# Attention and gated network on one core: a row of zeros for the maxima's products, and four groups of instructions in other places

## The chip, the cores and the metric

The kernel runs on one NeuronCore of a Trainium2 chip. The metric is the device time of one execution in microseconds; 677.85 us is the median of three runs (677.08 to 679.14). The engines have short names: PE is TensorE (PEld its weight loads), DVE VectorE, ACT ScalarE, POOL GpSimd, SP SyncE, which issues all transfers.

## The reference

For x of 4 x 512 x 512, the layer norm xn feeds two branches that are multiplied:

```
xn = (x - mean) / sqrt(var + 1e-5)
q, k, v = split(xn @ w_qkv)            # 16 heads of 32
q, k = rope(rmsnorm(q)*q_gamma), rope(rmsnorm(k)*k_gamma)
s = softmax(causal(q k^T / sqrt(32))) v @ w_out
f = (silu(xn Wg^T) * (xn Wu^T)) Wd^T   # hidden 1408, W = (int - 128)*scale
out = x + s * silu(f)
```

All of it is float32 in and out. The products on PE take a number as a high and a low part.

## The kernel before, in words

**Beats.** The middle of the program is 65 beats; beat c (0 to 63) does the attention of one head of one group of four heads: batch c // 16, group c // 4 % 4, head k = c % 4. Each engine has a written-out list of steps for a beat (`beat`), and goes through it in order; steps of different engines are tied by semaphores alone. In beat c, PE makes the transposed scores of head c in three operations (`scores_t`, L1383), the products with v of head c-1 and the first of head c (`p_v`, L1398), the products for the row maxima of block k of the next group (`maxima`, L1419, four heads), the projection of tile c+7 (`project`, L1358), the turns of tile c+5 (`turn`, L1370, for q and then k, both through one bank) and up to two halves of the gate and up products (`gate_half`, L1461).

**Maxima.** A softmax needs the maximum of a row first. q and k of a head stand as three parts of 32 rows each (KS = 96 rows) in `qst` and `kst`. The maxima's products use these 96 rows. Row 96 of `qst` holds the negated maxima, written there by SP's transfers `m0_out` and `m_out`, and row 96 of `kst` holds ones, so that the scores, with 97 rows, come out less the maximum. On DVE `maxima` (L1094) reduces a bank; PE may use a bank again when DVE is through with it.

**Statistics.** Where `ln_at` says so, DVE's beat has `ln_stats` (L1015 to L1021) and `ln_apply` (L1027) for one tile of the next batch, with POOL's power (L631) between them. They stand behind the last maxima of the beat and ahead of the sum of the rope (L1061) and of `p_low` of operation 2 (L1072). Before, they are in beats 2, 4, 6, 8 for batch 1, in 16, 18, 20, 22 for batch 2, in 32, 34, 36, 38 for batch 3. PE turns these tiles in beats 9 and 10 (batch 1), 23 to 26 and 39 to 42, whose output goes to both branches.

**Down products.** From beat 57 on PE also does `down`: 22 products a tile, two for each of 11 pieces m of the hidden size (L1486, L1487), into banks 0 to 3. `DOWN_AT` puts them at the end of a beat. In beats 55 to 58 PE also has the output projection of batch 2 (`out_proj`, L1437), 12 products in three parts through the same bank as the turns, so that the turn of q waits for ACT's `s_evac` (L811) and the turn of k for ACT's `q_evac` (L771).

**The ending.** Behind the beats PE does the rest of the down products, tiles n = 3 to 15 (n = 4b + t), and between them the four output projections of the last batch. The pieces of a tile become usable in chunks (four, four and three pieces): a load `hf_raw` by SP (L397), a high part on ACT (L853), a low part on DVE (L1140). DVE's order there is fixed too: low(9), scaled(0,2), o_low, low(10), scaled(0,3), finish(0,0), finish(0,1), low(11) and so on; low(10) and low(11) are the chunks of tile (1, 2) from m = 4 and from m = 8. A `finish` (L1279, L1281) needs its `xs` loads and a free half of `res`; SP then stores it.

## Time and profile before

| | |
|---|---|
| median of the runs | 677.85 us (677.08 to 679.14) |
| the profiled execution | 678.34 us, its span 676.6 us |
| PE, PEld | busy 652.6 us (96%), 551.5 us (82%) |
| DVE, ACT, POOL | busy 536.0 us (79%), 456.5 us (67%), 414.8 us (61%) |
| chain that ended last | PE 69%, DVE 11%, POOL 5%, issue 5%, DMA 5%, ACT 4% |
| granted clock, mean | 0.997 |
| DMA | 94.40 MB, 140 GB/s |

The span is the time from the first to the last instruction of one profiled execution; its 678.34 us holds 1.7 us more around it. The granted clock is the share of TensorE's full clock that it was given.

### The profile page before, as it was taken

How to read it: one execution, taken by the hardware profiler on the slowest of the kernel's cores; microseconds unless marked ns; L12 is line 12 of the kernel's file. 1: busy time of each engine (PE TensorE's matmuls, PEld its weight loads, DVE VectorE, ACT ScalarE, POOL GpSimd, SP SyncE). 2: the span in 40 equal slices, each digit the busy share in tenths (PEclk: the TensorE clock that was granted, in tenths of full speed). 3: DMA queues.
4: the chain of work that ended last, by engine and by line, in shares of the span. 5: the costliest groups of instructions: out<-in, count | busy, mean ns of one | idle time of the engine just before them, and what ended most of it. 6: DMA issues, size and time to landing. Idle time of an engine off the chain costs nothing.

```text
span 676.6 us, 12576 instructions
## 1 busy us (share of the span) xinstructions
PE 652.6 (96%) x3690; PEld 551.5 (82%) x3690; DVE 536.0 (79%) x1345; ACT 456.5 (67%) x1013; POOL 414.8 (61%) x591
## 2 busy tenths in 40 slices
PE   8889999999999999999999999999999989999997
PEld 7778888888888878888888888888888876777786
DVE  6786988998798888787988887878788866735857
ACT  3588787877676767776766677777677765741541
POOL 7968787787666667676666676766657673520000
PEclk9999999999999999999999999999999989999999
DMA  7546436332524341154343421244462515449896
GB/s 278 194 140 216 152 125 187 105 106 79 154 73 134 103 111 49 48 157 125 111 126 95 110 65 45 73 113 150 121 202 79 156 42 155 119 143 333 281 325 202
DMA packets 62591, 94.40 MB, mean 140 GB/s; under 512 B 12092, under 2 KB 24380, under 8 KB 62396
## 3 DMA queue, kind: packets, MB, share of 16 engines
q1 hardware_dynamic: 62524, 93.59, 45.0%
q8 instruction: 31, 0.51, 0.3%
q14 instruction: 36, 0.29, 0.2%
HBM read 59.09 MB, written 25.82 MB: 125 GB/s over the span
## 4 chain that ended last, share of the span: by engine, by line
PE 69%; DVE 11%; POOL 5%; issue 5%; DMA 5%; ACT 4%; SPq 1%; DVEq 0%; ACTq 0%; POOLq 0%
PE bank L1461 22%; PE bank L1358 16%; PE bank L1398 9%; PE bank L1419 5%; PE bank L1383 4%; PE bank L1370 4%; PE bank L1437 4%; DMA hf_raw<-hf_dram 2%; DVE bank L1094 2%; DVE ht_l L1140 2%; POOL rr L635 1%; ACT ht_h L853 1%; DMA out<-res 1%; PE bank L1486 1%; PE bank L1487 1%
## 5 line engine op out<-in xcount | busy, mean ns | idle before, releaser
L655 POOL TENSOR_SCALAR_AFFINE_SELECT pp<-pp 128x256 fp32r<-128x256 f32 x256 | 108.2, 435 | 141.1 <-DVE pp L1072 140.9
L1094 DVE CUSTOM_DVE_ANT_0 bank<-bank,msk_w 128x128 f32<-128x128 f32 (+3 forms) x256 | 121.3, 510 | 41.6 <-PE bank L1419 41.5
L1072 DVE TENSOR_TENSOR pp<-pf,pp 128x512 fp32r<-128x512 f32 (+1 forms) x192 | 135.4, 705 | 5.1 <-ACT pp L786 4.5
L635 POOL TENSOR_TENSOR rr<-ss,half 128x8 f32<-128x8 f32 x64 | 109.5, 1712 | 17.0 <-DVE ss L1040 17.0
L1358 PE MATMUL bank<-wq,xnt_h 128*128 128x384 f32 x512 | 111.7, 340 | 2.7 <-DVE qn L1052 2.4
L785 ACT ACTIVATE pf<-bank 128x512 f32<-128x512 f32 (+1 forms) x192 | 100.4, 523 | 19.5 <-PE bank L1383 17.3
L786 ACT ACTIVATE pp<-bank 128x512 fp32r<-128x512 f32 (+1 forms) x192 | 100.8, 525 | 0.0
L1461 PE MATMUL bank<-xnt_h,wgu 128*128 128x512 f32 x352 | 99.0, 403 | 0.7 <-DVE g L1118 0.7
L1398 PE MATMUL bank<-pp,va 128*65 128x512 f32 (+3 forms) x512 | 97.5, 311 | 1.0 <-POOL pp L655 1.0
L1461 PE MATMUL bank<-xnt_l,wgu 128*128 128x512 f32 x352 | 96.6, 396 | 0.0
L1358 PEld LDWEIGHTS bank<-wq,xnt_h 128*128 128x128 f32 x512 | 88.4, 188 | 6.0 <-issue 4.2
L1461 PEld LDWEIGHTS bank<-xnt_l,wgu 128*128 128x128 f32 x352 | 66.2, 188 | 16.3
L644 POOL TENSOR_TENSOR rb<-qn,sg 128x128 f32<-128x128 f32 x128 | 72.3, 585 | 0.0
L1419 PE MATMUL bank<-kst,qst 96*128 96x128 f32 (+3 forms) x256 | 71.2, 349 | 1.0 <-DVE mx L1094 0.8
L1486 PE MATMUL bank<-wd,ht_h 128*128 128x512 f32 (+1 forms) x187 | 70.9, 384 | 1.3 <-DVE ht_l L1140 1.1
L1398 PEld LDWEIGHTS bank<-pp,va 128*65 128x65 f32 x512 | 58.4, 136 | 16.8 <-POOL pp L655 1.4
L1487 PE MATMUL bank<-wd,ht_l 128*128 128x512 f32 (+1 forms) x187 | 70.6, 383 | 0.0
L1461 PEld LDWEIGHTS bank<-xnt_h,wgu 128*128 128x128 f32 x352 | 60.8, 188 | 11.4 <-issue 1.1
L1358 PE MATMUL bank<-wq,xnt_l 128*128 128x384 f32 x256 | 69.0, 352 | 0.0
L776 ACT ACTIVATE kst<-bank 96x512 fp32r<-96x512 f32 x64 | 38.0, 593 | 40.9 <-PE bank L1370 40.9
L771 ACT ACTIVATE qst<-bank 96x512 fp32r<-96x512 f32 x64 | 38.1, 595 | 39.1 <-PE bank L1370 39.0
L1370 PEld LDWEIGHTS bank<-idr,tt 128*96 128x96 f32 x512 | 49.0, 125 | 18.4 <-issue 3.8
(90 smaller groups left out, 1210.3 us busy)
## 6 DMA issues: line engine op xcount, KB each, us to landing
wgu<-wg_dram SPq DMA_DIRECT2D x66, 256.0 KB, 3.1
hf_dram<-g SPq DMA_DIRECT2D x44, 256.0 KB, 3.2
hf_raw<-hf_dram SPq DMA_DIRECT2D x16, 512.0 KB, 6.9
wg_dram<-wgu SPq DMA_DIRECT2D x22, 256.0 KB, 3.1
xr<-x SPq DMA_DIRECT2D x16, 256.0 KB, 4.6
oh<-oraw SPq DMA_DIRECT2D x64, 64.0 KB, 2.0
ol<-oraw SPq DMA_DIRECT2D x64, 64.0 KB, 2.0
s_dram<-s_sb SPq DMA_DIRECT2D x16, 256.0 KB, 2.7
```

Source lines behind the costliest of these rows:

```text
L635: pool.tensor_tensor(rr[:, s, :], ss[:, s, :], half[:], ALU.pow).then_inc(rr_ok, 1)
L655: op = pool.affine_select(pp[:, :, a:a + P], pp[:, :, a:a + P], [[0, 2], [1, P]], ALU.is_ge, 0.0, base=0, channel_multiplier=-1)
L785: act.activation(pf[:, tile], bank[:, 0:w], ACT.Exp, scale=SCALE)
L786: act.activation(ph[:, tile], bank[:, 0:w], ACT.Exp, scale=SCALE).then_inc(p_ok, 1)
L1072: dve.tensor_tensor(pl[:, tile], pf[:, tile], ph[:, tile].bitcast(F32), ALU.subtract).then_inc(pl_ok, 1)
L1094: op = dve.tensor_tensor_reduce(bank[:, a * w:(a + 1) * w], bank[:, a * w:(a + 1) * w], msk_w[:, N - w:N], 1.0, -3.0e38, ALU.add, ALU.max, ...
L1358: op = pe.matmul(qkv_bank(n)[:, 0:3 * GC], x_[:, k, t * P:(t + 1) * P], wq[:, g, w_, k, :], start=(a == 0), stop=(a == len(todo) - 1))
L1398: op = pe.matmul(PV_PS[0:VW, j * P:N], va[:, v, j, h, :], part[:, a:a + w], start=(j == 0 and part is ph), stop=(j == 2 and part is pl))
L1419: op = pe.matmul(bank[:, a * w:(a + 1) * w], qst[0:KS, par, h, qb * P:(qb + 1) * P], kst[0:KS, par, h, 0:w], start=True, stop=True)
L1461: op = pe.matmul(GU_PS[:], wgu[:, s, k, :], x_[:, k, :], start=(a == 0), stop=(a == len(todo) - 1))
L1486: pe.matmul(down_bank(t, part)[:, out_], ht_h[s][:, m, cols], wd[:, m, out_], start=(m == 0), stop=False)
L1487: op = pe.matmul(down_bank(t, part)[:, out_], ht_l[s][:, m, cols], wd[:, m, out_], start=False, stop=(m == MT - 1))
```

## The change

1. `KM = KS + 1`. Row 96 of `qst` becomes zeros (one transfer in the fill), rows 96 and 97 of `kst` ones, and the negated maxima go to row 97. The maxima's products take 97 rows (zero times one is added), the scores 98. PE waits for the zeros ahead of its first maxima.
2. `ln_at`: the statistics are in beats 4, 5, 7, 8 for batch 1, 12, 16, 20, 24 for batch 2, 28, 32, 36, 40 for batch 3; the load of the tiles is one beat earlier.
3. `DOWN_MID`: the four pieces of beat 57 and the four of beat 58 go in pairs ahead of the turn of q and ahead of the turn of k.
4. The four late output projections stand behind tiles 6 to 9, not 5 to 8, with ACT's and SP's steps for them; SP issues the first three chunks of batch 2 right behind the first `xs` loads.

```
+KM = KS + 1
+        DOWN_MID = {57: ((0, 0, 2), (0, 2, 4)), 58: ((0, 4, 6), (0, 6, 8))}
-        DOWN_AT = {57: ((0, 0, 4),), 58: ((0, 4, 8),), 59: ((0, 8, MT), (1, 0, 3)), 60: ((1, 3, 8),),
+        DOWN_AT = {59: ((0, 8, MT), (1, 0, 3)), 60: ((1, 3, 8),),
@@ ln_at
-            b, t = r + 1 + c // 16, c % 16 - (0 if c // 16 else 2)
-            t = t // 2 if t in (0, 2, 4, 6) else None
+            b = (c + 4) // 16 + 1
+            t = (c + 4) % 16 // 4 if c % 4 == 0 else None
+            if b == 1 or c == 0:
+                b, t = 1, {4: 0, 5: 1, 7: 2, 8: 3}.get(c)
@@ sync: m0_out, and m_out likewise; beat; fill; the ending
-                sp.dma_start(qst[KS:KS + 1, par, 0:1, :].bitcast(F32).rearrange(
+                sp.dma_start(qst[KM:KM + 1, par, 0:1, :].bitcast(F32).rearrange(
-                if c % 16 == 12 and there(c // 16 + 2, B):
+                if c % 16 == 11 and there(c // 16 + 2, B):
+                sp.wait_ge(zero_ok, 1)
+                sp.dma_start(qst[KS:KM, :, :, :].bitcast(F32).rearrange("o a h n -> o (a h) n"),
+                             pp[0:2 * HG, 0, 0:N].bitcast(F32)).then_inc(zr_in, 16)
                 load_w(1)
...
             for t in range(TB):
                 load_xs(0, t)
+            sp.wait_ge(dn_full, TB)
+            for v in range(NC):
+                load_hf(4 * NC + v)
...
-                    for v in range(2 * NC):
+                    for v in range(NC if b == 1 else 0, 2 * NC):
-                if TB + 1 < n <= 2 * TB + 1:
-                    s_store(B - 1, n - TB - 2)
+                if TB + 2 < n <= 2 * TB + 2:
+                    s_store(B - 1, n - TB - 3)
@@ gpsimd
-            pool.memset(kst[KS:KS + 1, :, :, :].bitcast(F32), 1.0).then_inc(ones_ok, 1)
+            pool.memset(kst[KS:KM + 1, :, :, :].bitcast(F32), 1.0).then_inc(ones_ok, 1)
@@ scalar: the ending
-                if TB < n <= 2 * TB:
-                    s_evac(B - 1, n - TB - 1, LATE_PS[n - TB - 1])
+                if TB + 1 < n <= 2 * TB + 1:
+                    s_evac(B - 1, n - TB - 2, LATE_PS[n - TB - 2])
@@ tensor: scores_t, maxima, beat, fill, the ending
-                    op = pe.matmul(bank[:, c0:c0 + w], kst[0:KS + 1, par, h, j * P:(j + 1) * P],
+                    op = pe.matmul(bank[:, c0:c0 + w], kst[0:KM + 1, par, h, j * P:(j + 1) * P],
...
-                        op = pe.matmul(bank[:, a * w:(a + 1) * w], qst[0:KS, par, h, qb * P:(qb + 1) * P],
-                                       kst[0:KS, par, h, 0:w], start=True, stop=True)
+                        op = pe.matmul(bank[:, a * w:(a + 1) * w], qst[0:KM, par, h, qb * P:(qb + 1) * P],
+                                       kst[0:KM, par, h, 0:w], start=True, stop=True)
+                if c in DOWN_MID:
+                    down(0, *DOWN_MID[c][0])
                 turn_q()
...
+                if c in DOWN_MID:
+                    down(0, *DOWN_MID[c][1])
                 if late_turn(c):
                     turn_k()
...
+                pe.wait_ge(zr_in, 16)
                 maxima(0, 0, (0,))
...
-                if TB < n <= 2 * TB:
-                    late = n - TB - 1
+                if TB + 1 < n <= 2 * TB + 1:
+                    late = n - TB - 2
```

How the order of instructions moves. On PE in beat 57, from the scores of operation 2 on (L1437 is the output projection, L1370 the turns, L1486 and L1487 the down products), before:

```order
L1383 MATMUL bank<-qst,kst 128x256
L1437 MATMUL bank<-wo_h,on 128x512
L1437 MATMUL bank<-wo_h,on_l 128x512 x3
L1370 MATMUL bank<-idr,tt 96x128 x8
L1486 MATMUL bank<-wd,ht_h 128x512
L1487 MATMUL bank<-wd,ht_l 128x512
L1486 MATMUL bank<-wd,ht_h 128x512
```

and in the changed kernel, where the same lines are L1393, L1447, L1380, L1496 and L1497:

```order
L1393 MATMUL bank<-qst,kst 128x256
L1447 MATMUL bank<-wo_h,on 128x512
L1447 MATMUL bank<-wo_h,on_l 128x512 x3
L1496 MATMUL bank<-wd,ht_h 128x512
L1497 MATMUL bank<-wd,ht_l 128x512
L1496 MATMUL bank<-wd,ht_h 128x512
L1497 MATMUL bank<-wd,ht_l 128x512
L1380 MATMUL bank<-idr,tt 96x128 x4
L1496 MATMUL bank<-wd,ht_h 128x512
L1497 MATMUL bank<-wd,ht_l 128x512
```

Two down pieces now stand ahead of the turn of q and two between the turns. On DVE in beat 7, from the last maxima to the next gate step (L1061 sums the rope, L1072 makes the low part of operation 2), before:

```order
L1094 ISA bank,mx<-bank,msk_w 128x512
L1094 ISA mx 128x1
L1061 TENSOR_TENSOR qp<-ra,rb 128x256
L1072 TENSOR_TENSOR pp<-pf,pp 128x256
L1040 TENSOR_REDUCE ss<-sq 128x8
L1123 SCALAR_TENSOR_TENSOR g<-bank,hsc,g 128x512
```

and in the changed kernel (L1104 maxima, L1071 rope, L1082 low part, L1050 squares, L1133 gate step):

```order
L1104 ISA bank,mx<-bank,msk_w 128x512
L1104 ISA mx 128x1
L1025 BN_STATS st<-xr 128x6
L1028 COPY st<-st 128x1
L1029 BN_AGGR mv<-st 128x2
L1031 TENSOR_SCALAR ve<-mv 128x1
L1071 TENSOR_TENSOR qp<-ra,rb 128x256
L1082 TENSOR_TENSOR pp<-pf,pp 128x256
L1037 TENSOR_SCALAR xr<-xr,mv,rstd 128x512
L1050 TENSOR_REDUCE ss<-sq 128x8
L1133 SCALAR_TENSOR_TENSOR g<-bank,hsc,g 128x512
```

The statistics of tile 2 have come between them from beat 6. On SP in the ending, from the last load of batch 0's `xs` on, before (L542 `xs`, L547 the stores, L397 the chunks):

```order
L542 DMA xs<-s_dram 128x512
L547 DMA out<-res 128x512
L542 DMA xs<-x 128x512
```

and in the changed kernel (L549, L401, L554):

```order
L549 DMA xs<-s_dram 128x512
L401 DMA hf_raw<-hf_dram 128x4x256 x2
L401 DMA hf_raw<-hf_dram 128x3x256
L554 DMA out<-res 128x512
L549 DMA xs<-x 128x512
```

The three chunks stood behind three stores before, and stand ahead of the first now.

## Rows read from the trace of the kernel before

**Rows 1.** Windows: length, busy PE, PEld, DVE, ACT, POOL (x), PEclk, DMA share, GB/s.
```profile
82.00:242.00 160.00, 157.86 (x937) 135.55 (x936) 138.83 (x373) 120.20 (x278) 115.95 (x164) 1.00 0.40 119
126.92:133.89 6.97, 6.14 (x45) 5.57 (x44) 6.50 (x19) 5.38 (x12) 4.28 (x7) 1.00 0.23 78
176.05:185.40 9.35, 9.35 (x54) 7.91 (x53) 7.53 (x19) 6.27 (x15) 5.56 (x10) 1.00 0.37 114
212.08:222.02 9.94, 9.61 (x54) 7.91 (x53) 8.57 (x23) 6.71 (x17) 6.80 (x11) 1.00 0.33 113
246.82:256.64 9.82, 8.95 (x54) 7.62 (x53) 8.72 (x24) 6.04 (x15) 7.19 (x10) 1.00 0.26 81
```

**Rows 2.** Groups by form on PE: form, count, busy us, mean ns, idle before.
```profile
L1419 PE MATMUL bank<-kst,qst 96*128 96x512 f32 x64 | 25.6, 438 | 0.8 <-DVE mx L1094 0.8
L1419 PE MATMUL bank<-kst,qst 96*128 96x384 f32 x64 | 21.1, 370 | 0.0
L1419 PE MATMUL bank<-kst,qst 96*128 96x256 f32 x64 | 14.3, 307 | 0.0
L1419 PE MATMUL bank<-kst,qst 96*128 96x128 f32 x64 | 10.3, 283 | 0.2 <-ACT kst L776 0.2
L1383 PE MATMUL bank<-qst,kst 97*128 97x512 f32 x64 | 25.4, 398 | 0.0
L1383 PE MATMUL bank<-qst,kst 97*128 97x384 f32 x64 | 21.7, 339 | 0.0
L1383 PE MATMUL bank<-qst,kst 97*128 97x256 f32 x64 | 19.2, 299 | 0.6 <-ACT pp L786 0.5
L1383 PE MATMUL bank<-qst,kst 97*128 97x128 f32 x64 | 14.3, 223 | 0.0
```

**Rows 3.** Timeline, PE, turn of beats 55 and 56: start us, length us, instruction.
```profile
535.91 0.41 PE L1370 MATMUL bank<-idr,tt 128*96 128x128 f32 x4
536.16 0.64 PE L1398 MATMUL bank<-pp,va 128*65 128x512 f32 x2
537.24 0.63 PE L1419 MATMUL bank<-kst,qst 96*128 96x128 f32 x4
537.71 0.51 PE L1398 MATMUL bank<-pp,va 128*65 128x384 f32 x2
```

**Rows 4.** Groups by form on DVE: the statistics and their application.
```profile
L1015 DVE BATCH_NORM_STATS2 st<-xr 128x6 f32<-128x512 f32 x16 | 11.0, 686 | 1.9 <-DMA xr<-x 1.9
L1027 DVE TENSOR_SCALAR xr<-xr,mv,rstd 128x512 f32<-128x512 f32 x16 | 9.9, 620 | 2.4 <-POOL rstd L607 0.9
```

**Rows 5.** Waits of PE between 545 and 566 us: total, times, longest.
```profile
PE bank L1370 <- ACT s_sb L811: 1.7, 2, 1.0
PE bank L1370 <- ACT qst L771: 1.1, 2, 0.8
```

**Rows 6.** Windows within beat 57, before and in the fall of the clock.
```profile
549.93:553.20 3.27, 1.51 (x11) 1.17 (x11) 2.92 (x5) 2.07 (x6) 3.27 (x5) 1.00 0.02 5
553.20:556.60 3.40, 3.40 (x10) 2.39 (x9) 0.71 (x2) 0.84 (x3) 1.76 (x2) 0.52 0.15 37
```

**Rows 7.** Timeline, PE, the first two late output projections.
```profile
608.24 1.17 PE L1437 MATMUL bank<-wo_h,on_h 128*128 128x512 f32 x4 [1.24 <-ACT on_h L799]
616.58 1.09 PE L1437 MATMUL bank<-wo_h,on_h 128*128 128x512 f32 x4
```

**Rows 8.** Timeline, DVE, two low parts of the ending and the tail.
```profile
609.08 1.22 DVE L1140 TENSOR_TENSOR ht_l<-hf_raw,ht_h 128x1024 fp32r<-128x1024 f32 x1 [0.26 <-ACT ht_h L853]
614.08 0.95 DVE L1140 TENSOR_TENSOR ht_l<-hf_raw,ht_h 128x768 fp32r<-128x768 f32 x1
671.08 0.69 DVE L1279 TENSOR_TENSOR res<-gt,xs 128x512 f32<-128x512 f32 x1 [1.59 <-DMA out<-res]
```

**Rows 9.** Waits of PE from 590 us on.
```profile
PE bank L1486 <- DVE ht_l L1140: 1.1, 2, 1.0
```

**Rows 10.** The page, DMA issues.
```profile
oh<-oraw SPq DMA_DIRECT2D x64, 64.0 KB, 2.0
```

More of the change, by code:

```diff
@@ L191, in build @@
         hf_raw = (hf_raw0, hf_raw1, hf_raw2, hf_raw3)
-        zero_ok = sem("zero_ok")
+        zero_ok, zr_in = sem("zero_ok"), sem("zr_in")
         id_in, c_in, msk_in = sem("id_in"), sem("c_in"), sem("msk_in")
@@ L442, in m_out @@
                 sp.wait_ge(mt_ok, 4 * r + c // 4 + 1)
-                sp.dma_start(qst[KS:KS + 1, par, 1:HG, :].bitcast(F32).rearrange(
+                sp.dma_start(qst[KM:KM + 1, par, 1:HG, :].bitcast(F32).rearrange(
                     "o h (t n) -> o (h t) n", t=TB), mrow[:].bitcast(F32)).then_inc(m_in, 16)
@@ L1382, in scores_t @@
                 for j, c0, w in ST_OPS[e]:
-                    op = pe.matmul(bank[:, c0:c0 + w], kst[0:KS + 1, par, h, j * P:(j + 1) * P],
-                                   qst[0:KS + 1, par, h, j * P:N], start=True, stop=True)
+                    op = pe.matmul(bank[:, c0:c0 + w], kst[0:KM + 1, par, h, j * P:(j + 1) * P],
+                                   qst[0:KM + 1, par, h, j * P:N], start=True, stop=True)
                 op.then_inc(st_full, 1)
```

## The prediction

> **What bounds the kernel now.** I read the windows first. From 82 to 242 us PE is busy 157.86 of 160 us and no other engine over 139 (the first row) [rows 1]. So in the beats the time is PE's list of products and how tightly they follow each other, and a product made shorter is time gained. The exceptions are in the same group: beat 9 (126.92 to 133.89), where PE is busy 6.14 of 6.97 us; beat 19 (212.08 to 222.02), 9.94 us long where beat 15 (176.05), with nearly the same products, takes 9.35; and beat 23 (246.82), where PE idles 0.87 of 9.82 us. Then the groups by form, to set the maxima's products beside the scores; then PE's waits and the clock in beats 57 and 58; then the ending, where the order of PE and the lateness of DVE's low parts decide.
>
> **The 97th row.** 256 products on PE change, 64 of each width. With 96 rows they take 438, 370, 307 and 283 ns for 512, 384, 256 and 128 columns; the scores, with 97 rows and the same widths, take 398, 339, 299 and 223 [rows 2]. The scores show no extra time where they precede or follow products of 128 rows, so I expect the maxima to become like them: 64 x (40 + 31 + 8 + 60) ns = 8.9 us. Durations of pipelined products overlap, so the starts are a second bound: four maxima of 128 columns take 0.47 us from the first start to the next group's (537.24 to 537.71), four turns of 128 columns and 128 rows take 0.25 (535.91 to 536.16), 0.055 us each more [rows 3]; on all 256 that is 14 us. The low end is 0, if the row count isn't the cause; a loss I exclude, since the scores carry a 97th row and are the shorter ones. I take 8.9 us, since the wide ones show less than the narrow ones. The scores go from 97 to 98 rows, at no cost: both lie within what the 97 rows already need beyond 96. The transfer of zeros is one of some 2.0 us [rows 10], issued in the fill among loads of much more, and its wait stands ahead of the first maxima, behind five tiles' projections; behind that wait all of PE's list is queued, so if the cover were gone it would cost the 2.0 us. SP's wait for the zeros in SBUF holds the load of weights behind it, for a clearing on which PE's first products wait anyway.
>
> The Trainium skill, page "TensorE: Matmul & The Clock Gate", section "LDWEIGHTS (loading the stationary operand)", says that a load takes its time from the columns and that fewer contraction rows don't change it, and its section "Why this matters for your kernels" gives a product of 32 rows the same time as one of 128. By that rule this term is 0. The rows of the trace disagree for products of 96 rows, and I go by the rows.
>
> **The statistics.** One tile costs DVE 0.69 us for the statistics and 0.62 for their application [rows 4], 1.3 us with the three small steps left out. Taken away: in beats 2, 18 and 34 they make DVE late for the heavy beat that follows; beat 19 is 9.94 - 9.35 = 0.59 us longer than beat 15, whose forerunner has none [rows 1]. Three such beats give 1.8 us. In beats 22 and 38 they stand before beats 23 and 39, where PE idles 0.87 us [rows 1]: 1.7 us. Added: tile 2 of batch 1 goes from beat 6 to beat 7, where DVE is loaded most, with beat 8's behind it and beats 9 and 10 ahead, in which PE waits for DVE already. Nothing there hides 1.3 us on DVE, so PE pays 1.3; at best 0, if DVE gains as much in beat 7 from what left beat 6. Beats 12 and 28 get one after a short beat; I put down 0.3 each, between 0 and 1.3. Queued behind the statistics on DVE are the rope's sum and the low part of operation 2, for which POOL's mask and PE's products wait a beat later. Beats 24 and 40 cost nothing: PE has output projections there and DVE half a beat's rest. Sum -3.5 + 1.9 = -1.6, between -3.5 and +1.7.
>
> **The down products of beats 57 and 58.** PE waits 1.7 us in two waits for ACT's copy of the output projection and 1.1 in two for the copy of the turned q [rows 5]. In each place now stand four products. A product of 512 columns takes (616.58 - 608.24 - 0.3) / 34 = 0.236 us (12 of the projection, 22 down, and a short wait between) [rows 7], so four take 0.94: as much as the longest wait. What they need (the last projection's bank, the first chunks) is there a beat before. 2.7 of the 2.8 us go. With them goes the reason for the fall of the clock: in 549.93 to 553.20 PE is busy 1.51 of 3.27 us, and in the 3.40 us that follow the granted clock is 0.52, that is the 1.2 GHz level for nearly all of it, in which PE loses (1 - 0.52) x 3.40 = 1.6 us [rows 6]. Sum -4.3, between -2.0 and -4.5. What is late next is POOL's mask for the products with v, some tenths behind.
>
> **The ending.** Before, PE is through with tile (1, 1) at 608.24 - 1.24 = 607.0 and waits for the last group's output, then does the projection, 12 x 0.236 = 2.8 us, then tile (1, 2), until 616.58 [rows 7]. Now tile (1, 2) starts at 607.0. Its pieces from m = 4 are at hand at 609.08 + 1.22 = 610.3, those from m = 8 at 614.08 + 0.95 = 615.0 [rows 8]; DVE's and ACT's order there, and the loads that this hangs on, don't change. So 8 products until 608.9, a wait of 1.4, 8 products until 612.2, a wait of 2.8, 6 products until 616.4. PE is where it was, without the 2.8 us of projection: +2.6. The waits of 1.1 us for low parts [rows 9], of which 1.0 is the start of tile (2, 0), go, since its chunks are now loaded three stores earlier: -1.0. DVE is then less behind, and its wait of 1.59 us for a store in the tail [rows 8] shrinks; 0.6 of it is on the end's path by my estimate (0 to 1.6). And from 608.9 to 615.0 PE would be busy 1.9 of 6.1 us, 31%, less than the 46% ahead of the fall in beat 57 [rows 6]: I expect the clock to fall here, for +1.6. Sum +2.6 - 1.0 - 0.6 + 1.6 = +2.6, between -1.6 (the low parts come sooner with a less crowded queue) and +3.5.
>
> **The sum.** -8.9 - 1.6 - 4.3 + 2.6 = -12.2 us, from 678.34 of the profiled execution: 666.1. That execution is 0.5 us over the median of the runs shown, so 665.6.
>
> **Rivals.** *The clock holds in the ending* (its fall in beat 57 is one event, and single waits of 1.2 us did not bring one): 1.6 less, 664.0. *DVE takes PE's place.* The beats get 0.14 us shorter each while DVE's work stays; in beats 7 to 12 and wherever DVE fills over 8.5 us it becomes the bound, and half of the 8.9 does not arrive: 670.1. For it speaks beat 19 [rows 1], against it the 21 us of DVE's rest in 160. *The row count is not the cause*: the maxima are long because each waits for a bank that DVE has just left. Then 8.9 us are missing: 674.5. Against it: products behind each other in one bank, with no wait between, are long as well [rows 3]. *Slower than before*: the two waits of the ending drop the clock to 1.2 GHz and it stays there through the following 55 us of down products, where PE is the bound; that would lose half, up to 27 us, and from 24 us of it the kernel is slower than 677.85: 680 or so. Against it: in beat 57 it came back within 3.40 us of dense products [rows 6]. *More than the durations show*: at the 14 us of the starts, 661.
>
> **Chances.** Forecast 0.45 (its own range 664.8 to 667.5), clock holds 0.22, DVE 0.18, row count 0.08, slower 0.02, more 0.05. The range 661 to 671.5 leaves out the row count, the slow case and the edges of the DVE case. A measurement of this kernel tells about 0.3%, 2 us, from no change; all cases but one lie further down: faster 0.97, same 0.01, slower 0.02.
>
> **What would show it.** By form: the maxima at 398, 339, 299 and 223 ns, within 10. Beats 19 and 35 at 9.4 us, 23 and 39 at 9.0, beats 9 and 10 together a us longer. No wait at the turns of beats 57 and 58, beat 57 near 7.8 us, clock 1.00. In the ending two waits for low parts in tile (1, 2), of over 1 and over 2 us, with a window of clock near 0.5 right behind, and none at tile (2, 0). I am wrong if the maxima keep their durations, if waits for DVE grow by over 4 us in the beats, or if tile (1, 2) finds its low parts ready.

## The result: 0.4% faster, where 1.8% was forecast

The changed kernel takes 674.91 us, median of 7 runs (674.32 to 676.46), against 677.14 for the kernel before in the same session (7 runs, 676.41 to 679.14). The ratio is 0.9963, 95% interval 0.9951 to 0.9975, so 1.7 to 3.3 us faster. The forecast was 665.6 us with a range from 661 to 671.5: the time lies outside it. The profiled execution took 675.65 us with a span of 673.9.

First the groups by form on PE, the question of the largest term. In this view a row has the form (rows * columns of the weights, then rows x width of the moving side), the count, the busy time, the mean ns and the idle time before:

```profile
L1429 PE MATMUL bank<-kst,qst 97*128 97x512 f32 x64 | 25.6, 438 | 0.8 <-DVE mx L1104 0.8
L1429 PE MATMUL bank<-kst,qst 97*128 97x384 f32 x64 | 21.2, 371 | 0.0
L1429 PE MATMUL bank<-kst,qst 97*128 97x256 f32 x64 | 14.3, 307 | 0.0
L1429 PE MATMUL bank<-kst,qst 97*128 97x128 f32 x64 | 10.3, 283 | 0.2 <-ACT kst L786 0.2
L1393 PE MATMUL bank<-qst,kst 98*128 98x512 f32 x64 | 25.6, 401 | 0.0
```

They answer to [rows 2]: the maxima now have 97 rows and take 438, 371, 307 and 283 ns, where they took 438, 370, 307 and 283 with 96. Not one nanosecond of 8.9 us came.

Then the windows (length, busy PE, PEld, DVE, ACT, POOL, granted clock, DMA share, GB/s): 160 us of beats, and beats 9, 15, 19 and 23, which answer to [rows 1]:

```profile
83.72:243.72 160.00, 157.84 (x934) 135.06 (x933) 137.96 (x378) 120.07 (x276) 114.02 (x164) 1.00 0.41 117
129.10:136.07 6.97, 6.27 (x46) 5.57 (x45) 6.67 (x19) 5.39 (x13) 4.41 (x7) 1.00 0.24 78
178.40:187.80 9.40, 9.40 (x55) 7.94 (x54) 7.53 (x19) 6.28 (x15) 5.58 (x10) 1.00 0.38 121
214.47:223.86 9.39, 9.39 (x55) 7.93 (x54) 7.28 (x19) 6.68 (x16) 5.59 (x10) 1.00 0.39 111
248.70:257.48 8.78, 8.78 (x55) 7.66 (x54) 7.12 (x19) 6.01 (x15) 6.38 (x9) 1.00 0.30 85
```

PE is as full as before. Beat 9 has its old length, beat 19 is now 9.39 us long (9.94 before), beat 23 8.78 (9.82 before), and PE no longer idles in it.

In beats 57 and 58 the waits of [rows 5] are gone: between 545 and 566 us PE's waits are two of 0.2 us. Beat 57 takes 7.80 us instead of 11.24, beat 58 7.73 instead of 9.34. The place of the fall of the clock in [rows 6] reads 1.00. The fall stands elsewhere now, twice: in the fill, and in the ending. The rows are beat 57, the fill, and the ending before and in its fall:

```profile
553.00:556.50 3.50, 3.50 (x21) 2.97 (x20) 2.82 (x7) 3.03 (x8) 1.86 (x3) 1.00 0.18 40
44.50:48.00 3.50, 3.50 (x12) 2.79 (x11) 2.02 (x7) 1.44 (x5) 2.14 (x2) 0.51 0.45 150
604.90:611.10 6.20, 3.33 (x13) 2.44 (x14) 4.79 (x8) 1.98 (x3) 0.00 (x0) 1.00 1.06 384
611.20:614.60 3.40, 3.40 (x10) 2.64 (x9) 0.00 (x0) 0.00 (x0) 0.00 (x0) 0.50 1.09 376
```

The ending answers to [rows 7 to 9]. First PE's timeline at its two waits in tile (1, 2) and the projection behind them, then ScalarE's (ACT) and VectorE's (DVE) at the same place (start, length, instruction, in brackets the idle time before it and what ended it), then PE's waits from 584 us on (total, times, longest):

```profile
604.98 0.50 PE L1496 MATMUL bank<-wd,ht_h 128*128 128x512 f32 x1 [1.51 <-DVE ht_l L1150]
609.91 0.50 PE L1496 MATMUL bank<-wd,ht_h 128*128 128x512 f32 x1 [2.79 <-DVE ht_l L1150]
611.61 1.91 PE L1447 MATMUL bank<-wo_h,on_h 128*128 128x512 f32 x4
```
```profile
601.94 0.63 ACT L809 ACTIVATE on_h<-on 128x512 fp32r<-128x512 f32 x1 [2.52 <-POOL on L678]
602.61 1.06 ACT L863 ACTIVATE ht_h<-hf_raw 128x1024 fp32r<-128x1024 f32 x1
603.70 1.23 DVE L1150 TENSOR_TENSOR ht_l<-hf_raw,ht_h 128x1024 fp32r<-128x1024 f32 x1 [0.40 <-ACT ht_h L863]
606.22 0.69 DVE L1289 TENSOR_TENSOR res<-gt,xs 128x512 f32<-128x512 f32 x1 [0.70 <-DMA xs<-s_dram]
607.00 0.63 ACT L869 ACTIVATE gt<-yt 128x512 f32<-128x512 f32 x1 [3.34 <-DVE res L1289]
607.54 0.83 ACT L863 ACTIVATE ht_h<-hf_raw 128x768 fp32r<-128x768 f32 x1
608.90 0.95 DVE L1150 TENSOR_TENSOR ht_l<-hf_raw,ht_h 128x768 fp32r<-128x768 f32 x1
```
```profile
PE bank L1496 <- DVE ht_l L1150: 4.5, 3, 2.8
```

Both waits have a queue behind them. The second chunk's high half on ACT (602.61) stands in order behind the copy of the last normalized block, which waits 2.52 us for POOL. The third chunk's low half on DVE (608.90) stands behind the residual sums of tiles (0, 0) and (0, 1), which wait for a DMA. Its high half on ACT (607.54) is queued too: it stands behind an activation that waits 3.34 us for the first of these sums. PE's four projections then take 1.91 us instead of 1.17, the clock having fallen.

The account of the profiled executions, by the start of beats: beat 0 starts 1.40 us later (47.16 against 45.76), beats 0 to 62 take 534.11 instead of 541.03 us (-6.92), and from beat 63 to the end it is 92.64 instead of 89.83 (+2.81). The sum is -2.7 us, as the spans say. The +2.81 are +3.6 until PE's last product and -0.8 from there to the end (4.26 us instead of 5.04).

### The profile page after: what moved, and what is told of

Its sections match the earlier page's. It is cut to its first block, busy times and chain, and to the rows that moved or that the text cites. A ratio compares the mean times of both kernels' runs of the same rounds, so it can differ in the third digit from the quotient of the medians.

```text
span 673.9 us, 12577 instructions
## 1 busy us (share of the span) xinstructions
PE 653.6 (97%) x3690; PEld 553.1 (82%) x3690; DVE 531.5 (79%) x1345; ACT 456.9 (68%) x1013; POOL 412.3 (61%) x591
## 4 chain that ended last, share of the span: by engine, by line
PE 81%; DVE 5%; POOL 5%; ACT 3%; issue 3%; DMA 2%; SPq 1%; ACTq 0%; DVEq 0%; POOLq 0%
PE bank L1471 23%; PE bank L1368 17%; PE bank L1408 9%; PE bank L1447 6%; PE bank L1429 6%; PE bank L1393 5%; PE bank L1497 4%; PE bank L1496 4%; PE bank L1380 4%; POOL rr L645 1%; DMA stage<-w_qkv 1%; DVE bank L1104 1%; POOL pp L665 1%; DVE pp L1082 1%; DMA xs<-s_dram 1%
## 5 line engine op out<-in xcount | busy, mean ns | idle before, releaser
L1104 DVE CUSTOM_DVE_ANT_0 bank<-bank,msk_w 128x128 f32<-128x128 f32 (+3 forms) x256 | 121.3, 509 | 38.2 <-PE bank L1429 37.8
L1082 DVE TENSOR_TENSOR pp<-pf,pp 128x512 fp32r<-128x512 f32 (+1 forms) x192 | 133.0, 693 | 5.0 <-ACT pp L796 4.4
L1496 PE MATMUL bank<-wd,ht_h 128*128 128x512 f32 (+1 forms) x187 | 70.3, 381 | 4.5 <-DVE ht_l L1150 4.5
L1429 PE MATMUL bank<-kst,qst 97*128 97x128 f32 (+3 forms) x256 | 71.3, 350 | 1.0 <-DVE mx L1104 0.8
L1497 PE MATMUL bank<-wd,ht_l 128*128 128x512 f32 (+1 forms) x187 | 70.3, 382 | 0.0
L1380 PEld LDWEIGHTS bank<-idr,tt 128*96 128x96 f32 x512 | 49.1, 125 | 15.2 <-issue 2.4
```

Of the source, the lines that this page charges most:

```text
L1082: dve.tensor_tensor(pl[:, tile], pf[:, tile], ph[:, tile].bitcast(F32), ALU.subtract).then_inc(pl_ok, 1)
L1104: op = dve.tensor_tensor_reduce(bank[:, a * w:(a + 1) * w], bank[:, a * w:(a + 1) * w], msk_w[:, N - w:N], 1.0, -3.0e38, ALU.add, ALU.max, ...
L1429: op = pe.matmul(bank[:, a * w:(a + 1) * w], qst[0:KM, par, h, qb * P:(qb + 1) * P], kst[0:KM, par, h, 0:w], start=True, stop=True)
L1496: pe.matmul(down_bank(t, part)[:, out_], ht_h[s][:, m, cols], wd[:, m, out_], start=(m == 0), stop=False)
L1497: op = pe.matmul(down_bank(t, part)[:, out_], ht_l[s][:, m, cols], wd[:, m, out_], start=False, stop=(m == MT - 1))
```

## The experiments

Each is measured beside the kernel before on the same chip. The interval in brackets is that of the ratio. Of each edit only the main lines are shown.

**The parts one by one.** The row of zeros alone:

```
+KM = KS + 1        # maxima 97 rows, scores 98, statistic in row KM
+                sp.dma_start(qst[KS:KM, :, :, :]..., pp[0:2 * HG, 0, 0:N]...).then_inc(zr_in, 16)
```


> The kernel before with the row of zeros alone (scores 98 rows, maxima 97 rows, the statistic of the maxima moved to row 97, the transfer of zeros in the fill and the wait for it). Theory of the prediction (rows set the pace of a maxima product): the 512-wide maxima fall from 438 to about 400 ns and the kernel is 8.9 us faster. Theory now (the row count sets nothing; what is slow is the product that stands behind a 128-wide one, whatever its rows): maxima products stay at 438, 371, 307 and 283 ns within 5 ns, and the time is the one before, or up to 1.6 us longer if the clock falls in the fill at 44 to 48 us as in the changed kernel. If the clock does not fall in the fill here, the row of zeros is not its cause, and the loss of 1.4 us before beat 0 belongs to another part.

Measured: 677.96 against 677.16 us, ratio 1.0006 (0.9993 to 1.0020). The durations:

```profile
L1423 PE MATMUL bank<-kst,qst 97*128 97x512 f32 x64 | 25.6, 438 | 0.8 <-DVE mx L1098 0.8
L1423 PE MATMUL bank<-kst,qst 97*128 97x128 f32 x64 | 10.3, 283 | 0.2 <-ACT kst L780 0.2
```

The part does nothing to the products. The clock didn't fall in the fill in this execution. It did in that of the late projections alone (below), where the row is left out, so the row of zeros is not needed for the fall:

```profile
44.50:47.90 3.40, 3.40 (x12) 2.75 (x10) 2.01 (x8) 1.44 (x4) 1.99 (x2) 0.51 0.47 154
```

The statistics alone:

```
-            t = t // 2 if t in (0, 2, 4, 6) else None
+            t = (c + 4) % 16 // 4 if c % 4 == 0 else None
+            if b == 1 or c == 0:
+                b, t = 1, {4: 0, 5: 1, 7: 2, 8: 3}.get(c)
```


> The kernel before with the places of the statistics alone (and the load of the next block's rows one beat earlier). My forecast of this part was 1.6 us faster; the lengths of beats in the trace of the changed kernel against those of the kernel before now say about 2.3 us faster (beats 3, 19, 35 each 0.5 to 0.6 and beats 23, 39 each 1.0 to 1.1 shorter, beat 6 longer by 1.0, beats 8, 13, 29 by 0.2 each). If that reading is right, 1.8 to 2.8 us come off with the statistics alone; the rival, that the gains of the changed kernel come from the row of zeros and its shorter waits, expects under 1 us here.

Measured: 676.77 us, ratio 0.9984 (0.9967 to 1.0001), that is 1.1 us faster, between 2.2 faster and 0.1 slower: by the runs alone not clear of no change. The beats that changed are those of the changed kernel to 0.04 us: 3, 19 and 35 shorter by 0.50 to 0.62, 23 and 39 by 1.05 and 1.09, beat 6 longer by 0.92, beats 8, 13, 29 by 0.17 to 0.19, in sum -2.4. So the gains belong to the statistics and not to the row, as the first theory had it. One beat runs against it: beat 60 is 0.84 us longer in this execution, with a wait of 0.7 us of its scores for the transfer of the maxima. That wait is absent in the changed kernel, so it isn't the statistics' own, but it leaves 1.5 us over the beats. The median's smaller gain also fits its runs' lower clock, 0.9959 in the mean against 0.9979 (the table below).

The down products alone:

```
+        DOWN_MID = {57: ((0, 0, 2), (0, 2, 4)), 58: ((0, 4, 6), (0, 6, 8))}
+                if c in DOWN_MID:
+                    down(0, *DOWN_MID[c][0])
                 turn_q()
```


> The kernel before with the down products of beats 57 and 58 in four pieces inside the beats alone. Forecast 4.3 us faster; the trace of the changed kernel says 5.0 us over beats 57 and 58, with no stretch at half clock at 553 to 557. Expected here: 4.3 to 5.1 us faster, clock fall of 553 to 557 gone. The rival, that the waits come back in beats 59 to 63 (VectorE is what feeds them), expects under 2.5 us.

Measured: 673.75 us, ratio 0.9947 (0.9928 to 0.9965), 2.4 to 4.9 us faster, the largest part, though its 3.6 us lie under the 4.3 to 5.1 that I expected. Beats 57 and 58 are 7.79 and 7.76 us. Beat 59 is 0.66 us longer than before, and 0.5 of it is a wait of the scores for the transfer of the maxima:

```profile
PE bank L1384 <- DMA qst<-mrow: 0.5, 1, 0.5
```

Other executions with the new order have this wait with 0.3 to 0.7 us, the changed kernel's has none, and the statistics alone have it in beat 60 with the old order. So I can't put it down to the down products. It is far less than the rival asked for.

The ending alone, with ACT's and SP's steps and the three early loads:

```
-                if TB < n <= 2 * TB:
-                    late = n - TB - 1
+                if TB + 1 < n <= 2 * TB + 1:
+                    late = n - TB - 2
```


> The kernel before with the ending alone: the last block's output projections one tile later, their evacuations and stores with them, and the three early loads of block 2's halves. Forecast 2.6 us slower, and the trace of the changed kernel says 2.7 us: TensorE waits for VectorE's low halves in the second and third tile of the ending (1.5 and 2.8 us, in place of 1.1 and 2.0), and the clock is halved for about 3.4 us behind them. If the projections' move is what does it, this kernel is 2.2 to 3.2 us slower than before and shows a stretch at half clock in the ending. The rival, that the early end of beats 57 and 58 is what makes VectorE late in the ending (it has the same work in less time), expects this kernel within 1 us of the one before.

Measured: 679.83 us, ratio 1.0035 (1.0017 to 1.0052), 1.2 to 3.5 us slower. PE's waits in its trace after 588 us:

```profile
PE bank L1489 <- DVE ht_l L1143: 4.1, 3, 2.2
```

The waits come with this part alone; that beats 57 and 58 end earlier isn't needed for them. In this execution the clock held in the ending in spite of them, so the stretch at half clock that I expected was not seen here; its one fall before the end was in the fill.

The other way round, the changed kernel with the projections where they were; the early loads stay:

```
-                if TB + 1 < n <= 2 * TB + 1:
-                    late = n - TB - 2
+                if TB < n <= 2 * TB:
+                    late = n - TB - 1
```


> The changed kernel with the output projections of the ending where they were before (one tile earlier); all else of the change stays, the row of zeros among it. If the parts add up as measured one by one (later projections 2.4 us slower), this is 672.5 us, within 671.5 to 673.5. If the ending of the changed kernel is slow for another reason (VectorE late from beats 57 and 58), it is within 0.7 us of the changed kernel's 674.9.

Measured: 670.95 us, ratio 0.9917 (0.9897 to 0.9936). By the ratios that is 3.1 us under the changed kernel (4.0 by the medians of the two sessions), and 1.5 us better than I expected from the single parts. The 2.4 us of the ending alone are the move and the early loads together, the 3.1 are the move alone; the intervals are too wide to read the loads' worth from the difference. PE waits 1.1 us once in its ending, for the last normalized block:

```profile
PE bank L1447 <- ACT on_h L809: 1.1, 1, 1.1
```

So more than half of what the other parts gained, 5.6 us by this ratio, was given back by this one; with both intervals, the move cost about 1.5 to 4.7 us.

**What makes the maxima long.** The two scores of the second operation exchanged, in the kernel before:

```
-ST_OPS = [[(0, 0, 512)], [(1, 0, 384), (3, 384, 128)], [(2, 0, 256)]]
+ST_OPS = [[(0, 0, 512)], [(3, 384, 128), (1, 0, 384)], [(2, 0, 256)]]
```


> The kernel before with the two products of the second scores operation exchanged: the 128-wide one (queries of block 3) first, the 384-wide one behind it. Theory now (a product is late by 0.05 to 0.07 us when it loads 128 columns of weights behind a 128-wide product): the 512- and 384-wide maxima that stand directly behind the scores fall from 443 to about 398 ns and from 388 to about 341 ns, and the 384-wide score, now behind the 128-wide one, rises from 337 to about 385 ns; the time stays within 1.5 us of the one before. Rival (a maxima product is long by itself, by its 96 rows or because VectorE is still reading the neighbouring bank): maxima stay at 443 and 388 ns, scores at 337.

Measured: 677.54 us, ratio 1.0008 (0.9986 to 1.0031). By form:

```profile
L1383 PE MATMUL bank<-qst,kst 97*128 97x384 f32 x64 | 24.9, 389 | 0.0
L1419 PE MATMUL bank<-kst,qst 96*128 96x512 f32 x64 | 24.8, 426 | 0.8 <-DVE mx L1094 0.8
L1419 PE MATMUL bank<-kst,qst 96*128 96x384 f32 x64 | 20.4, 359 | 0.0
L1383 PE MATMUL bank<-qst,kst 97*128 97x128 f32 x64 | 14.3, 224 | 0.0
```

The 384-wide scores, always fast before (339 ns), are long now (389), because now they stand behind the 128-wide one. The maxima have become shorter without a change to their operands, by 12 ns in the mean of 64: a quarter of them stood directly behind the scores. Sorted by what stands ahead, the 512-wide maxima behind the scores go from 443 ns to 395, and those behind another 512-wide maximum stay (397 and 395). Beat 19's start shows one of these, first in the changed kernel, then in this one:

```profile
214.47 0.63 PE L1393 MATMUL bank<-qst,kst 98*128 98x512 f32 x3
214.94 0.44 PE L1429 MATMUL bank<-kst,qst 97*128 97x512 f32 x1
```
```profile
212.75 0.68 PE L1383 MATMUL bank<-qst,kst 97*128 97x512 f32 x3
213.27 0.39 PE L1419 MATMUL bank<-kst,qst 96*128 96x512 f32 x1
```

Three scores 0.63 us and the maximum 0.44; exchanged, 0.68 and 0.39. The 0.05 us belongs to the product that follows a 128-wide one, whichever that is. It was moved, not removed, and the time stayed. DVE reads the same banks in both kernels, so its reading isn't the cause.

The maxima with 96 instead of 128 columns of weights (the maxima of 32 queries in each block left out):

```
-    pe.matmul(bank[:, a * w:(a + 1) * w], qst[0:KS, par, h, qb * P:(qb + 1) * P],
+    pe.matmul(bank[0:KS, a * w:(a + 1) * w], qst[0:KS, par, h, qb * P:qb * P + KS],
```


> The kernel before with maxima of 96 query columns instead of 128 as the stationary operand (the maxima of 32 queries in each block are left out); rows, moving widths and order are as before. Theory now (loading 128 columns takes about 0.11 us, which a 128-wide product of 0.06 us does not cover): the group of four 128-wide maxima goes from a spacing of about 0.11 us to about 0.07 to 0.09, its products from 276 ns to about 240, and the maxima behind a 128-wide product fall by 0.02 to 0.04 us; those behind a 384- or 512-wide product stay at 341 and 398 ns. Rival (rows or VectorE's reading of the bank): nothing changes in these durations. The time: 0 to 1 us under the one before, too little to tell.

Measured: 675.97 us, ratio 0.9990 (0.9970 to 1.0009).

```profile
L1419 PE MATMUL bank<-kst,qst 96*96 96x512 f32 x64 | 24.7, 424 | 0.8 <-DVE mx L1094 0.8
L1419 PE MATMUL bank<-kst,qst 96*96 96x384 f32 x64 | 20.3, 358 | 0.0
L1419 PE MATMUL bank<-kst,qst 96*96 96x256 f32 x64 | 13.5, 295 | 0.0
L1419 PE MATMUL bank<-kst,qst 96*96 96x128 f32 x64 | 8.8, 261 | 0.2 <-ACT kst L776 0.2
```

With the same rows and fewer columns all four forms get shorter, by 12 to 22 ns. The gain sits behind the narrow products: behind the 128-wide score the 512-wide maximum goes from 443 to 419 ns, behind another 512-wide one it stays (397 and 398). The time's interval holds both no change and 2 us, as I had said it would be too small to tell. The group of four 128-wide maxima at the head of beat 20, PE and then the weight loads (PEld), in the changed kernel and in this one:

```profile
224.35 0.64 PE L1429 MATMUL bank<-kst,qst 97*128 97x128 f32 x4
224.32 0.53 PEld L1429 LDWEIGHTS bank<-kst,qst 97*128 97x128 f32 x4
```
```profile
221.55 0.56 PE L1419 MATMUL bank<-kst,qst 96*96 96x128 f32 x4
221.52 0.45 PEld L1419 LDWEIGHTS bank<-kst,qst 96*96 96x96 f32 x4
```

Over all such groups the starts of neighbouring 128-wide products are in the median 113 ns apart with 128 columns of weights and 96 or 97 rows, 109 with 128 columns and 128 rows (the transposes of x), 87 with 96 columns, 59 with 65 columns (the products with v). Columns set the pace of these products, rows don't. A 128-wide product passes in 59 ns or less; the load of 128 columns for the next one takes about 110, and the 50 ns between them show as lateness of that next one. Behind a product 256 wide or wider the load is covered: a 256-wide maximum takes 281 ns behind another 256-wide one and 332 behind the 128-wide score, a 512-wide maximum 397 to 399 ns behind a 384- or 512-wide product.

**What is worth keeping.** Down products and statistics, with batch 1's statistics at other beats and the early loads; the row and the late projections left out:

```
-                b, t = 1, {4: 0, 5: 1, 7: 2, 8: 3}.get(c)
+                b, t = 1, {1: 0, 4: 1, 6: 2, 8: 3}.get(c)
```


> What should be left of the change: the down products of beats 57 and 58 in pieces, the statistics at new places (those of batch 1 in beats 1, 4, 6 and 8 instead of 4, 5, 7 and 8, because the trace of the statistics alone shows beat 6 1.0 us longer), the early loads of block 2's halves; the row of zeros and the later output projections are left out. From the single parts measured (down 3.6 off, statistics 1.1 to 2.4 off and 0.9 more if beat 6 is as before) I expect 671.5, within 670 to 673; if VectorE's lateness simply comes back in the ending (rival), 673.5 or more, like the down products alone.

Measured: 670.01 us, ratio 0.9906 (0.9887 to 0.9925). I expected 671.5 from the single parts, within 670 to 673; as with the projections put back, the parts together gave 1.5 us more than their sum. Beat 6 is back at 8.99 us; beat 2 is 0.28 longer. PE's waits after 588 us:

```profile
PE bank L1443 <- ACT on_h L805: 1.5, 1, 1.5
PE bank L1492 <- DVE ht_l L1146: 0.2, 1, 0.2
```

On the same kernel, the first maxima of each beat behind the products with v, which load 65 columns:

```
-                banks(SM_A)
                 if k:
                     w_bank(0)
...
                     p_v(r, c - 1, 2)
+                banks(SM_A)
```


> The same kernel with the first maxima of each beat (the four 128-wide ones, or the first wider one) moved from behind the scores to behind the two value products of the beat before, whose weights are 65 columns wide. Theory now: the product behind the 128-wide score then loads 65 columns and is not late (the value product behind it stays at 408 or less), and the first maxima fall from 443 to about 400 ns; up to 60 times 0.05 = 3 us off against the kernel without this move, if VectorE, which gets these maxima about 1.5 us later, does not make TensorE wait for its low parts (that rival: 0 to 4 us slower, with waits for VectorE in front of the value products at the beat's end). Theory of rows: no product gets shorter and nothing is gained.

Measured: 678.62 us, ratio 1.0025 (1.0012 to 1.0039), 8.6 us slower than the kept version. By form between 183 and 320 us the 512-wide maxima take 418 ns against 436 in the kept version, the 128-wide ones 263 against 283. The v product that now stands behind the 128-wide score and loads 65 columns takes 341 ns, as behind wide ones (336): the mechanism is right. But these are PE's largest waits from 47 to 588 us, here and in the kept version:

```profile
PE bank L1404 <- POOL pp L661: 3.0, 6, 0.8
PE bank L1364 <- DVE qn L1058: 3.0, 5, 1.3
PE bank L1422 <- DVE mx L1100: 2.9, 4, 0.9
```
```profile
PE bank L1364 <- DVE qn L1058: 2.0, 3, 1.0
PE bank L1404 <- POOL pp L661: 0.9, 3, 0.3
```

The chain through DVE starts later and PE pays more for it than it saves: 18 of 63 beats get 0.2 to 0.9 us longer, and the beats together 7.8 us. The rival held, at twice the size that I gave it. The lists of waits, with their smaller rows, account for 5.2 us of this; the rest isn't traced.

**The queue in the ending.** Late projections again, on the kept version, with the second and third chunk's high halves on ACT and low halves on DVE ahead of what they stood behind, and SP's load of the second chunk ahead of the reciprocals' way back. ACT's lines:

```
             high(9)
-            o_high(LAST, G - 1)
             high(10)
-            outer(0, 2)
+            o_high(LAST, G - 1)
             high(11)
+            outer(0, 2)
```


> The kept version (670.0 us) with the later output projections of the changed kernel put in again, and three queues put in the order that these need: ScalarE makes the high halves of the second and third chunk of tiles (1,2), (1,3) ahead of the last normalized block's evacuation and the activations, VectorE makes their low halves ahead of the last block's low part and of the residual sums, SyncE issues the second chunk's load ahead of the last reciprocals' way back. Theory (the ending was slower because these products wait in order behind work that itself waits for GpSimd and for a DMA): the waits of 1.5 and 2.8 us in tile (1,2) go, TensorE no longer waits 1.5 us for the last normalized block either, and the time is 668.5, 1.5 us under the kept version. Rival (the loads of the second and third chunk are what comes late; they are issued at about 597 us): the waits in tile (1,2) stay at 1 us or more, and the time is 670.5 to 672.5. Up to 1 us is added if the clock falls behind such a wait.

Measured: 670.11 us, ratio 0.9904 (0.9885 to 0.9922), not the 668.5 that I expected: no faster than the kept version (0.9906, and 0.9894 when it was run again). The wait for the second chunk is gone, that for the third is 1.28 us instead of 2.79, and it stands behind the same copy as the second's did before:

```profile
602.41 0.63 ACT L805 ACTIVATE on_h<-on 128x512 fp32r<-128x512 f32 x1 [2.44 <-POOL on L674]
602.95 0.83 ACT L859 ACTIVATE ht_h<-hf_raw 128x768 fp32r<-128x768 f32 x1
604.83 0.50 PE L1492 MATMUL bank<-wd,ht_h 128*128 128x512 f32 x1 [1.28 <-DVE ht_l L1146]
```

With the third chunk ahead of it as well, on ACT and DVE, and its load on SP:

```
             high(10)
+            high(11)
             o_high(LAST, G - 1)
-            high(11)
```


> The kernel with the reordered ending, but now the third chunk of tiles (1,2), (1,3) too goes ahead of the last normalized block on ScalarE and VectorE, and its load ahead of the last reciprocals' way back on SyncE. The trace of the kernel before this step shows the one wait that is left in the ending, 1.28 us at 604.8 in tile (1,2) for the third chunk's low halves, behind an evacuation on ScalarE that starts at 602.4 when GpSimd is done. Theory: that wait goes to under 0.3 us and the time is 668.9, 1.1 to 1.3 us under the kept version on the same chip. Rival (the reciprocals' way back, now behind one more load, makes the last block late and TensorE waits for it in front of the output projections instead): 1 us or more of waiting for ScalarE there, and no gain.

Measured: 670.56 us, ratio 0.9909 (0.9892 to 0.9926), where I expected 668.9. That wait is gone, PE's only ones from 585 us on are

```profile
PE bank L1492 <- DVE ht_l L1146: 0.5, 2, 0.3
```

and the stretch from beat 63 to the end is 87.10 us against 87.85 and 87.98 in the kept version's two profiles. The time doesn't show these 0.8 us; here is the kept version again on the same chip:

> The kept version once more, beside the one above on the same chip: 670.0, within 0.7 us of its first time.

Measured: 669.63 us, ratio 0.9894 (0.9875 to 0.9912). By the medians the kernel with the late projections is 0.9 us slower than this, within the noise. That the waits go when the order of the queues and of one load, then two, is changed is shown. The queues and the loads were not changed apart; for the queues speaks that in the changed kernel both high halves start right behind other work on ACT and don't wait for a load. That the late projections are worth anything without the waits isn't shown.

**The clock.** The kept version's two profiles differ by 1.5 us in the span with the same instructions. The same stretch of the fill in the first and in the second:

```profile
44.00:47.50 3.50, 3.50 (x18) 2.98 (x19) 3.24 (x10) 2.85 (x6) 2.51 (x2) 1.00 0.32 110
```
```profile
44.00:47.50 3.50, 3.50 (x9) 2.79 (x10) 2.08 (x7) 1.93 (x4) 2.49 (x3) 0.51 0.38 105
```

So the fall in the fill, and the one in beat 57 of the kernel before, come in some executions and not in others: in the profile of the row of zeros alone beat 57 ran at full clock and took 9.74 us, not 11.24. Over the profiled executions of all kernels here, the fall in the fill is in 5 of 14. The one in beat 57 is in 3 of the 6 with the old order of the down products and in none of the 8 with the new one. The one in the ending is in that of the changed kernel alone. Mean granted clock and times, over the runs:

| kernel | runs | mean clock | mean us of the runs at 0.997 (how many) |
|---|---|---|---|
| before, beside the experiments | 79 | 0.9979 | 677.7 (30) |
| changed | 7 | 0.9944 | 674.5 (1) |
| row of zeros | 12 | 0.9974 | 678.2 (5) |
| statistics | 12 | 0.9959 | 675.9 (3) |
| down products | 6 | 0.9982 | 674.8 (1) |
| late projections | 12 | 0.9962 | 679.8 (2) |
| changed, projections not late | 6 | 0.9978 | 671.4 (3) |
| kept version | 6 | 0.9975 | 670.5 (3) |
| kept version, again | 5 | 0.9982 | 671.0 (1) |
| kept, late projections, first order | 6 | 0.9987 | 671.1 (1) |
| kept, late projections, second order | 6 | 0.9973 | 670.4 (4) |

The kernel before takes 675.8 us in its 20 runs at clock 1.000 and 678.3 in its 12 at 0.996. The changed kernel has the lowest clock in this table, lower by 0.0035 than the kernel before, or 2.4 us of a span of 675, and without its late projections it has 0.9978. That fits a fall behind the waits in tile (1, 2) in about every execution, as part of that term's price; only one execution was profiled, so it isn't shown.

## Why the prediction was wrong, step by step

**The 97th row: the step that failed.** I put down -8.9 us because the maxima "with 96 rows" are long and "the scores, with 97 rows and the same widths" short [rows 2], and expected the former to become like the latter. The premise of the comparison was wrong: the two groups differ in what stands ahead of them as much as in rows. Measured is 0 or 1 ns in each form, and +0.4 us (-0.5 to +1.4) with the row alone. The lateness is that of a load of 128 columns behind a 128-wide product (the exchanged scores and the 96 columns). My sentence that scores show no extra time wherever they stand was not read from a row. In operations 0 and 1 they are never behind a 128-wide product, and in operation 2 they are at times: 353 ns behind a turn, 282 behind a wide product, which a mean of 299 [rows 2] hides. The comparison in [rows 3], four maxima in 0.47 us against four turns in 0.25, was of products with 128 and with 96 columns of weights; I named the rows as the difference and did not see the columns. They are part of it: maxima with 96 columns stand 87 ns apart, between 113 and the turns' 62.

The Trainium skill, page "TensorE: Matmul & The Clock Gate", section "LDWEIGHTS (loading the stationary operand)", which I weighed and set aside, says that the time of a load goes by the columns and not by the rows, and an estimate from its time per column is 107 ns for 128 columns and 80 for 96. The maxima agree: nothing for the 97th row, 113 ns for 128 columns, 87 for 96. The turns, at 62 ns with 96 columns, don't agree with the 80.

My rival "the row count is not the cause" gave 674.5 us, 0.4 from the result, and I gave it 0.08; its own mechanism (a bank that DVE has just left) fell with the exchanged scores.

**The statistics: right, a little better than said.** Forecast -1.6, in the trace -2.3 by beats, measured alone -1.1 (-2.2 to +0.1) at a lower clock than before's, so the forecast's size rests on the beats and not on the median. The gains were 1.7 us in beats 3, 19 and 35 (forecast 1.8) and 2.1 in beats 23 and 39 (forecast 1.7). Of the costs I put 1.3 us on beats 9 and 10, for tile 2 in beat 7; nothing happened there. Instead beat 6 became 0.96 longer, behind tile 1's statistics in beat 5, for which I had no term: their application takes 1.52 us of DVE there, where it takes 0.64 to 0.66 in the other beats. Why it does isn't traced. At beats 1, 4, 6, 8 most of it goes.

**The down products: right.** Forecast -4.3, in the trace -5.05, alone -3.6 (-4.9 to -2.4). The size depends on whether the clock falls in beat 57 in the execution that one compares with: it did in the profile that I worked from. Without the fall beats 57 and 58 took 19.0 us before and take 15.5 now: 3.5 for the waits, where I had 2.7. The waits that I called the reason for the fall don't bring it every time: the row of zeros alone has them, and its clock held.

**The ending: the waits right, the sum in part luck.** The two waits are 1.5 and 2.8 us (forecast 1.4 and 2.8), the clock is at half behind them, there is no wait at tile (2, 0), together +2.8 against +2.6. Alone it measured +2.4 (1.2 to 3.5). Two of its terms hang on the execution. The clock held behind waits of 1.70 and 2.24 us in that of the ending alone, where I had +1.6. And the -1.0 for the early loads can't be credited to them: the wait of 0.97 us at tile (2, 0) is missing as well in the executions of the statistics alone, the down products alone and the exchanged scores, which don't have these loads. The tail did get shorter, by 0.8 us where I had 0.6: it is 4.25 to 4.27 us in all eight executions with the early loads, 4.43 to 5.16 in the six without. I had the chain too: "DVE's and ACT's order there ... don't change". What I did not draw from it is that this order, not the loads, was the limit.

**The start of beat 0**, 1.4 us later, no step foresaw; it is a fall of the clock in the fill. The kept version's second execution has it and its first doesn't, with the same instructions. The 0.3 us by which beat 0 itself is longer belong to it too.

Without the failed term the sum is -12.2 + 8.9 = -3.3 us, against -2.7 in the profiles and -2.5 in the ratio. That it comes so near is luck in part: the statistics and the down products gave 1.5 us more in the profiles than I had, and the fall in the fill took about as much away.

## What to carry to other kernels

Before a difference between two groups of products is put down to their shape, sort each group by what stands ahead of it: a mean over both kinds of neighbour carried the whole of an 8.9 us term here. In this kernel a 128-wide product makes the next one late when that one loads 128 columns of weights; behind the score belongs a product with few columns, or the order is left alone if another engine waits for the result of what would have to move. When work is moved later so that it no longer waits, look at the strict queues of the engines that feed what now comes earlier: its inputs stood behind exactly the work that was moved away from.

## What the runs showed of the hardware that I had not expected

The clock falls at the same few places (the fill, from 43 to 45 us; beat 57, from 552 to 554 us; the ending, behind the waits) in some executions of one kernel and not in others, and one fall costs 1.5 to 1.6 us (11.24 against 9.74 in beat 57, 47.71 against 46.13 to the start of beat 0): 0.2% of this kernel, more than two of the four parts measured. Twelve runs of one kernel (the row of zeros alone) spread over 3.8 us; its four runs at 0.999 and 1.000 are among its five fastest.

The pace of narrow products doesn't follow the columns of weights alone. With 96 columns it is 87 ns for maxima of 96 rows, and 62 ns for turns of 128 rows. What makes the turns faster no run here tells. Nor is the lateness behind them explained by the load alone: a 512-wide maximum takes 443 ns behind the 128-wide score and 465 to 469 behind a turn of q or k, and even a 512-wide v product, which loads 65 columns, takes 412 to 414 ns behind such a turn and 393 to 394 behind another v product.
